# Rank-one attention with keys on partitions: the weighted sums go from VectorE to TensorE

## The reference, cut to what matters

```python
x_avg = jnp.mean(x, axis=(2, 3), keepdims=True)
se_mid = jax.nn.relu(conv1x1(x_avg, se1_w, se1_b))
W_cw = jax.nn.sigmoid(conv1x1(se_mid, se2_w, se2_b))     # a gate per image and channel
g_x = conv1x1(x, g_w, g_b).reshape(b, N)                 # one channel each
theta_x = conv1x1(x, theta_w, theta_b).reshape(b, N)
phi_x = conv1x1(x, phi_w, phi_b).reshape(b, N)
f = theta_x[:, :, None] * phi_x[:, None, :]              # rank one
y = jnp.einsum('bij,bj->bi', jax.nn.softmax(f, axis=-1), g_x)
W_y = conv1x1(y.reshape(b, 1, h, w), W_w, W_b)
inv = bn_gamma / jnp.sqrt(bn_var + BN_EPS)
W_y = (W_y - bn_mean) * inv + bn_beta                    # per channel
return W_cw * W_y + x
```

## Time and profile before

| | |
|---|---|
| median of 3 runs (lowest, highest) | 2871.19 us (2867.90, 2873.26) |
| the profiled execution, its span | 2870.26 us, 2868.5 us |
| busy share of the span: PE, DVE, ACT, POOL | 95%, 76%, 58%, 3% |
| rank-one stage, from its first instruction to the end of the span | 2802.3 to 2868.5 us, 66.2 us |

### The profile page before, as it was taken

One profiled execution on the slowest core, in us unless ns is written; L12 is line 12 of the kernel. 1 busy time (PEld: TensorE's weight loads), 2 busy tenths in 40 slices (PEclk: granted clock), 3 DMA queues, 4 the chain that ended last, 5 costly groups with the idle time before them and its releaser, 6 DMA issues. The chain is left out here.

```text
span 2868.5 us, 45618 instructions
## 1 busy us (share of the span) xinstructions
PE 2717.4 (95%) x19977; PEld 1355.9 (47%) x19977; DVE 2182.4 (76%) x1415; ACT 1672.2 (58%) x2588; POOL 100.4 (3%) x65
## 2 busy tenths in 40 slices
PE   7399999999999999999999999999799999999893
PEld 3334444444444444334444344344578888757551
DVE  5499999999999999999999999998542221234447
ACT  2467776777777767777677777766522222211335
POOL 0000000000000000000000000000440000000004
PEclk9699999999999999999999999999899999999996
DMA  1100000000000000000000000000600000200001
GB/s 69 41 23 22 23 29 9 29 29 16 29 13 32 29 9 29 22 23 29 9 29 29 16 29 18 27 5 1 195 1 0 1 1 2 82 0 1 0 1 59
DMA packets 37607, 72.24 MB, mean 25 GB/s; under 512 B 20960, under 2 KB 21920, under 8 KB 35744
## 3 DMA queue, kind: packets, MB, share of 16 engines
q1 hardware_dynamic: 37344, 69.19, 7.2%
q0 software_dynamic: 64, 0.13, 0.0%
HBM read 60.45 MB, written 8.86 MB: 24 GB/s over the span
## 5 line engine op out<-in xcount | busy, mean ns | idle before, releaser
L734 PE MATMUL l_ps<-mlp_w,W2H 128*64 128x512 f16 x8192 | 1366.5, 392 | 17.2 <-DVE mlp_w L768 17.2
L768 DVE TENSOR_TENSOR mlp_w<-words_x,words_y 128x2048 f32<-128x2048 f32 x512 | 1159.5, 2287 | 66.9 <-PE l_ps L734 66.9
L734 PE MATMUL l_ps<-mlp_w,W2L 128*64 128x512 f16 x4096 | 802.3, 388 | 0.0
L734 PEld LDWEIGHTS l_ps<-mlp_w,W2H 128*64 128x64 f16 x8192 | 455.2, 108 | 549.3 <-issue 116.4
L815 ACT ACTIVATE relu_bottom<-l_ps 128x512 f32<-128x512 f32 x1024 | 612.3, 598 | 79.5 <-PE l_ps L734 1.4
L815 ACT ACTIVATE mlp_w<-l_ps 128x512 f32<-128x512 f32 x684 | 408.8, 598 | 279.7 <-PE l_ps L734 249.7
L752 DVE SCALAR_TENSOR_TENSOR mlp_w<-relu_bottom,sign_ratio,mlp_w 128x2048 f32<-128x2048 f32 x171 | 401.4, 2347 | 7.6 <-ACT relu_bottom L815 7.6
L734 PEld LDWEIGHTS l_ps<-mlp_w,W2L 128*64 128x64 f16 x4096 | 229.0, 109 | 179.7 <-issue 0.8
L815 ACT ACTIVATE relu_top<-l_ps 128x512 f32<-128x512 f32 x340 | 203.2, 598 | 135.7 <-PE l_ps L734 120.8
L723 PE MATMUL l_ps<-y_rows,y_weights_halves 12*128 12x512 bf16 x2048 | 202.4, 385 | 12.1 <-DMA y_rows<-y_pieces 12.1
L752 DVE SCALAR_TENSOR_TENSOR relu_top<-relu_bottom,sign_ratio,relu_top 128x2048 f32<-128x2048 f32 x85 | 199.6, 2349 | 4.0 <-ACT relu_bottom L815 4.0
(11 more groups left out here) (343 smaller groups left out, 2578.8 us busy)
## 6 DMA issues: line engine op xcount, KB each, us to landing
table_pos<-pos_table SPq DMA_DIRECT2D x64, 512.0 KB, 3.6
mlp_w<-in_mlp_w SPq DMA_DIRECT2D x8, 1024.0 KB, 14.0
X<-in_x SPq DMA_DIRECT2D x8, 512.0 KB, 7.6
bias_scratch<-bias_rows SPq DMA_DIRECT2D x64, 64.0 KB, 2.0
mlp_w_hi<-bias_scratch SPq DMA_DIRECT2D x16, 256.0 KB, 3.8
out<-Q SPq DMA_DIRECT2D x8, 512.0 KB, 2.7
y_rows<-y_pieces SPq DMA_DIRECT2D x192, 12.0 KB
xn_b<-in_out_wT SPq DMA_DIRECT2D x1, 1024.0 KB, 6.9
```

What stands on the lines that cost most here:

```text
L734: last = nc.tensor.matmul(out[q][a * DH:(a + 1) * DH, :], w[:, half], h[a][:, :, k], start=False, stop=stop, tile_position=(0, a * DH))
L768: nc.vector.tensor_tensor(hw[i % 3][:, r].rearrange("p (m j) -> p m j", j=J), words_x, words_y[:, 2 * n + r].unsqueeze(1).to_broadcast([P, ...
```

## The change

The rank-one stage is written anew. Keys now stand on partitions, 128 at a time (a round r of 8: 4 per image, as 128 keys of each quarter), and queries lie along the row, 512 at a time. In words:
- The argument of the exponential is a product of TensorE: two rows of keys (phi, and a one) times two rows of queries (theta, and the negative maximum). A round has four such products of 128 x 512, in four row groups of the array; each pair of them fills a double bank, `args`.
- ScalarE takes the exponential of a double bank (128 x 1024) straight from PSUM, without scale, bias or sum, 16 in all.
- The sums over keys are products too, of 32 columns (g, theta, phi, and a row of ones), in four column groups. They add up over the 4 rounds of an image in one bank.
- At the end of an image its bank is copied to SBUF, turned by four transposes, VectorE adds the halves and divides, and four products spread y.
- The largest argument comes from the extremes of phi over rows (two reductions, one set of small products), and `min` of two products of the queries.
- The averages of X are taken in the stage before, by ScalarE: of image 0 in four copies of 128 x 1024, of image 1 in eight of 128 x 512, each behind VectorE's addition. The normalization's coefficients move to the head of the stage before; the sigmoid is made of an exponential and a reciprocal.
- GpSimd only prepares the selecting matrices. VectorE shifts X (8 operations of 128 x 1024) and makes all outputs, in halves of 512 pixels; 16 stores of 256 KB.

The diff, cut to what the prediction speaks of:

```diff
@@ stage_nonlocal, vector: ahead of its own coefficients
+            dve.wait_ge(cs, 2)
+            nc.vector.reciprocal(K.bn_t[:], K.bn_a[:]).then_inc(bn, 1)
...
@@ stage_nonlocal, scalar: in the tail of image 1, and behind the loop
+                            for c in range(2 * t, 2 * t + 2):
+                                act.wait_ge(o_out, NT * CC)
+                                nc.scalar.activation(ex[c % 2], K.X[:, c, 0], ACT.Copy, accum_out=K.av[:, c, 0:1]).then_inc(mean, 1)
+                                act.wait_ge(mean, c + 1)
+                        act.wait_ge(z_mm, b * NT + t + 1)
                         nc.scalar.activation(z[:, t * BANK:(t + 1) * BANK], zps[t][:], ACT.Copy).then_inc(z_out, 1)
+            for i in range(NT * CC):
+                t, c = divmod(i, CC)
+                act.wait_ge(o_out, (B - 1) * NT * CC + i + 1)
+                act.wait_ge(mean, CC + i)
+                nc.scalar.activation(ex[2][:, 0:BANK], K.X[:, c, B - 1, t * BANK:(t + 1) * BANK], ACT.Copy,
+                                     accum_out=(K.av_b[:, c:c + 1] if t else K.av[:, c, 1:2])).then_inc(mean, 1)
@@ stage_rank_one, tensor
+            nc.tensor.matmul(args[0][:, 0], sel_q[:, 0], rows, start=True, stop=True).then_inc(qk_mm, 1)
+            nc.tensor.matmul(args[0][:, 1], sel_k[:, 0], rows, start=True, stop=True).then_inc(qk_mm, 1)
+            pe.wait_ge(ends, 2)
+            for n in range(B * NT):
+                last = nc.tensor.matmul(pps[:, 2 * n:2 * n + 2], sel_m[:, n], mm[:], start=True, stop=True)
...
+            nc.tensor.matmul(gps[:], sel_q[:, 1], rows, start=True, stop=True).then_inc(qk_mm, 1)
+            nc.tensor.matmul(args[2][:, 1], sel_k[:, 1], rows, start=True, stop=True).then_inc(qk_mm, 1)
...
+            def arguments(r):
...
+                for t in range(NT):
+                    k = NT * r + t
+                    if k >= 3:
+                        pe.wait_ge(ex, k - 2)
+                    for u in range(2):
+                        at = 32 * (2 * t + u)
+                        last = nc.tensor.matmul(args[k % 3][:, u], keys[b][at:at + 2, jj * P:(jj + 1) * P], queries[b][at:at + 2, :],
+                                                start=True, stop=True, tile_position=(at, 0))
+                    last.then_inc(a_mm, 1)
+            def weigh(r):
...
+                for t in range(NT):
+                    k = NT * r + t
+                    pe.wait_ge(ex, k + 1)
+                    for u in range(2):
+                        at, n = 32 * (2 * t + u), 32 * (NT * b + u)
+                        last = nc.tensor.matmul(acc[b][at:at + 32, :], rows_t[:, jj, n:n + 32], e[k % EB][:, u],
+                                                start=(jj == 0), stop=(jj == JJ - 1), tile_position=(0, at))
+                last.then_inc(s_mm, 1)
+            def replicate(b, t):
+                pe.wait_ge(col, 4 * (b + 1))
+                if b == 0 and t:
+                    pe.wait_ge(o_out, CC)
+                for r in range(JJ):
+                    last = nc.tensor.matmul(y_ps(b, t)[:, r * P:(r + 1) * P], num[:, b, r, t:t + 1].to_broadcast([P, P]), K.k("ident"),
+                                            start=True, stop=True)
+            for r in range(B * JJ):
+                arguments(r)
+                if r:
+                    weigh(r - 1)
+                if r == JJ + 1:
+                    columns(0)
+                if r == JJ + 2:
+                    replicate(0, 0)
+            weigh(B * JJ - 1)
+            replicate(0, 1)
+            columns(1)
+            for t in range(NT):
+                replicate(1, t)
@@ stage_rank_one, scalar
+            for k in range(TILES):
+                act.wait_ge(a_mm, k + 1)
+                if k >= EB:
+                    act.wait_ge(s_mm, (k - EB) // NT + 1)
+                nc.scalar.activation(e[k % EB], args[k % 3][:], ACT.Exp).then_inc(ex, 1)
@@ stage_rank_one, vector: behind the loop
+            dve.wait_ge(s_mm, JJ)
+            nc.vector.tensor_copy(sums[0], gps[:]).then_inc(s_out, 1)
+            quotient(0)
+            outputs(0, 0)
+            outputs(0, 1)
+            quotient(1)
+            outputs(1, 0)
+            outputs(1, 1)
```

More of the change, by code:

```diff
@@ L1590, in stage_rank_one @@
     d = K.dram
-    se1, se2 = K.se1, K.se2
+    se1, se2, av = K.se1, K.se2, K.av
     room = carver(K.WR)
[L1593 to L1597, removed]
-    gw = sb("gtp_w32", [P, CC, 32])
-    sel = sb("row_select", [P, 2, B * NT, P])
-    th = sb("theta", [P, B * PC])
-    av, mid, gate = sb("avg", [P, CC, B]), sb("se_mid", [SE, B]), sb("gate", [P, CC, B])
@@ L1610, in stage_rank_one @@
[L1610 to L1622, removed]
+    EB, JJ = 6, BANK // P
+    TILES = 2 * B * JJ
+    e = [room([P, 2, BANK]) for _ in range(EB)]
@@ new lines, in stage_rank_one @@
+    rows, rows_t = room([P, BANK]), room([P, JJ, P])
+    queries, keys = [room([P, BANK]) for _ in range(B)], [room([P, BANK]) for _ in range(B)]
+    scaled = [room([P, BANK]) for _ in range(B)]
+    sums = [room([P, BANK]) for _ in range(B)]
+    sel_q, sel_k, sel_m = room([P, B, P]), room([P, B, P]), room([P, B * NT, P])
+    out = carver(K.Q)([P, CC * B, HW])
+    gw = sb("gtp_w32", [P, CC, 32])
+    mid, gate = sb("se_mid", [SE, B]), sb("gate", [P, CC, B])
+    ga, gd = sb("ga", [P, CC, B]), sb("gd", [P, CC, B])
@@ L1677, in _ @@
             last.then_inc(se, 1)
[L1678 to L1682, removed]
+            def arguments(r):
+                b, jj = divmod(r, JJ)
+                pe.wait_ge(q_out, b + 1)
+                pe.wait_ge(k_out, b + 1)
+                for t in range(NT):
+                    k = NT * r + t
+                    if k == 1:
+                        pe.wait_ge(ends, 4)
+                    if k == 2:
+                        pe.wait_ge(t_out, 1)
+                        pe.wait_ge(k_out, 2)
+                    if k >= 3:
[5 more added lines that the diff above has]
+                    last.then_inc(a_mm, 1)
@@ L1747, in _ @@
[L1747 to L1758 removed]
+            dve.wait_ge(g_out, 1)
@@ new lines, in outputs @@
+            def outputs(b, t):
+                dve.wait_ge(y_mm, NT * b + t + 1)
+                dve.wait_ge(xg, CC * (b + 1))
+                part = slice(t * BANK, (t + 1) * BANK)
+                for c in range(CC):
+                    nc.vector.scalar_tensor_tensor(out[:, CC * b + c, part], y_ps(b, t), ga[:, c, b:b + 1], K.X[:, c, b, part],
+                                                   ALU.mult, ALU.add).then_inc(o_out, 1)
+            dve.wait_ge(s_mm, JJ)
+            nc.vector.tensor_copy(sums[0], gps[:]).then_inc(s_out, 1)
@@ L1760, in _ @@
+            quotient(0)
[4 more added lines that the diff above has]
+            outputs(1, 1)
         @block.scalar
         def _(act):
-            nc.scalar.activation(inv[:], K.v("bn_var", 0, CC), ACT.Sqrt, bias=K.eps[:]).then_inc(sq, 1)
-            for i in range(CC * B // 2, CC * B):
-                c, b = divmod(i, B)
-                last = nc.scalar.activation(out[i], K.X[:, c, b], ACT.Copy, accum_out=av[:, c, b:b + 1])
@@ L1767, in _ @@
-            last.then_inc(av_act, 1)
-            act.wait_ge(g_mm, 1)
-            nc.scalar.activation(rows, gps[:], ACT.Identity, bias=K.v("gtp_b")).then_inc(g_out, 1)
-            for i in range(2 * B * NT):
-                b, r = divmod(i, 2 * NT)
-                k, t = divmod(r, NT)
-                act.wait_ge(rep_mm, i + 1)
-                nc.scalar.activation(rep[:, k, b, t * BANK:(t + 1) * BANK], rps[i % 2][:], ACT.Copy).then_inc(rep_out, 1)
+            act.wait_ge(head, 3)
+            act.wait_ge(g_mm, 1)
```

242 lines of the change are left out of this document (125 added, 117 removed).

## The result

| | before | changed |
|---|---|---|
| median of 12 runs each (lowest, highest) | 2869.07 us (2866.95, 2873.26) | 2862.17 us (2859.09, 2868.12) |
| ratio of changed to before, 95% interval | | 0.9978 (0.9970 to 0.9986) |
| the profiled execution, its span | 2870.26 us, 2868.5 us | 2868.04 us, 2866.2 us |
| rank-one stage in the trace | 66.2 us | 57.4 us |

The forecast was 2850.5 us. The change gains, but a third of what was expected. The traces are compared by the length of the stage: where it begins also depends on the three layers ahead, which run the same instructions but for the coefficients and averages, and yet differ between executions by some us (the changed one is 2.2 us behind the one before at the end of the first layer, 2009 us, and 5.8 us from 2054 us on). The profiled execution of the changed kernel, at 2868.04 us, is one of the two longest of its twelve.

The account below looks back on a forecast made before the run. VectorE was taken to bound the loop and ScalarE most of the head. The stage takes 44.9 instead of 66.2 us and begins 0.75 later: 2870.26 - 20.5, plus 0.9 for the median, stated as 2850.5 us; range 2844 to 2864.

Parts of the forecast that it names:

- The start: Stage before: the last average of image 1 lets the rank-one stage begin 0.75 us later; bounds 0 to 5 us.
- The head: Stage's start to first exponential: it starts at 11.3 us, where before it was 20.3; clock left at 1.00.
- The loop's products side by side: Loop: four products of a kind overlap, about 0.86 us, not 3.44 one by one; 2.0 us per round.
- rival B: Loop at half the pace, by the second pair's wait or TensorE at 1.2 GHz: 3.6 us a round, 2863.5; chance 0.22.
- rival C: Loop: row groups don't overlap in float32, arguments 3.44 us a round, no gain, 2870.5; chance 0.06.
- The clock there: Loop: TensorE's granted clock taken as 1.00, as it would be busy 1.9 of 2.0 us.
- Rival D: Loop: both causes of rival B at once, 7.1 us a round, slower at 2891; chance 0.09.
- The insertions: Rounds 5 and 6: image 0's transposes and first spreading find no slack and add 1.8 us.
- The tail: Last sums at 30.1 us to stage's end at 44.9: spreadings, image 1's quotient, outputs of 2.75 and 5.4, store 2.75.
- The sum: Whole stage: 44.9 instead of 66.2 us, beginning 0.75 later, 20.5 us less; 2850.5 us forecast.

Follow-up runs that it names:

- e12: Changed kernel with argument products over 32 rows (30 of zeros) instead of 2 in all rounds, same edit as e1; 2851.34 us, ratio 0.9935 to the kernel before.
- e6: Changed kernel with argument products over 32 rows in rounds 0 to 3 (image 0), 2 rows in rounds 4 to 7; 2850.71 us, run once.
- e11: Changed kernel with argument products over 32 rows in rounds 0 and 1, 2 rows in rounds 2 to 7; 2851.91 us, ratio 0.9938 to the kernel before.
- e1: Changed kernel with argument products over 32 rows (30 of zeros) instead of 2 in all rounds; 2850.76 us, ratio 0.9935 to the kernel before.
- e3: Changed kernel plus one bf16 product over the full array ahead of each round's first pair, arguments still 2 rows; 2863.37 us, ratio 0.9986 to the kernel before.
- e8: Changed kernel with argument products over 32 rows in round 0 alone, 2 rows in rounds 1 to 7; 2863.07 us, ratio 0.9968 to the kernel before.
- e9: Changed kernel with argument products over 2 rows in rounds 0 and 1, 32 rows in rounds 2 to 7; 2854.44 us, run once.

## Why the prediction was wrong, step by step

- *The start*, 0.75 later: 0.74. Right.
- *The head*, first exponential at 11.3: 12.03. The first products end at 4.18 (4.15 forecast). Most of the miss is the small products of line 1694: they hold TensorE 0.81 us from their start to that of the next line (2815.74 to 2816.55), where 0.3 had been taken. The full products were 0.2 longer than forecast and the gate's layer 0.2 shorter. GpSimd was done after 3.25 us (4), and the clock stayed at 1.00 as forecast.
- *The loop's products side by side*: right. In the changed kernel's full rounds all four argument products start within 0.02 us, the wait ahead of the second pair notwithstanding, so the first cause of rival B and rival C are refuted. At the high clock a round's arguments take 1.07 us, or 1.24 where the second pair waits for its exponential, and its sums 1.0 (e12), turns included, where 0.96 each had been summed.
  The Trainium skill, "TensorE: Matmul & The Clock Gate", Part 3, with its 3.07 for four row tiles, gave an estimate of 1.12 us without the turn; e12's rows have 1.07 with the turn in it, where no wait lengthens them.
- *The clock there*, "TensorE will be busy 1.9 of 2.0 us, so I take 1.00". **This is the step that failed.** It was 0.50 for 27 us, and a round took 3.89 instead of 2.0. Rival B named this as its second cause, and said 2863.5 us against the 2862.2 measured. The cost is e12's difference from the changed kernel: 11.0 us in the trace, 10.8 between the medians. The reasoning failed where it read busy time as the clock's measure. The row taken as the model, the first layer's alternation, has argument-like products over 12 rows and a clock of 1.00. It stood next to the right answer: e6 and e11 show that such an alternation does keep a high clock. But the loop's entry doesn't alternate, and its four products over two rows, twice over, were never looked at by themselves. Rival D's own line, that such products are little work, was the better argument.
  The Trainium skill, "TensorE: Matmul & The Clock Gate", Part 1, What's actually happening, says that the clock is set by how busy TensorE has been of late. Busy time as the profile shows it doesn't bear this out: 27.20 of 27.20 us at 0.50 in the changed kernel, 17.20 of 20.10 at 1.00 in e11.
- *The insertions*, 1.8 in all: in e12 the transposes and the spreading delay the exponentials by some 0.7 and 1.0 us. Right. The last exponential ends at 30.6 in e12 (29.1 forecast), of which 0.7 is the head's.
- *The tail*, 14.8 us from the last sums to the end: 13.7 in the changed kernel, since the clock had risen by then and the spreading took 1.17 instead of 1.7. In e12, where the clock is low there as forecast, it is 14.7.
- *The sum*: with wide products all terms hold to 1.5 us together (stage 46.4 for 44.9), and the time is 2850.8 for 2850.5. Of the 11.7 us by which the forecast missed, 10.8 are the clock. That the time agrees to 0.3 us is in part luck: the forecast was taken off a median of 2871.2 us from three runs, and the twelve gave 2869.1. The gain with wide products is 17.4 to 17.6 us (e12, e1), not 20.5. In the traces the stage is 19.8 us shorter and begins 0.74 later; for the rest, the first layer's products start 0.8 to 2.4 us later in all 14 traces of changed kernels than in the one before, and one trace before can't tell whether that is the kernel's or the execution's. The range, 2844 to 2864, held because B was in it.
- One thing in the text ahead of the forecast was imprecise: a round takes 128 keys from each half of the image, for each half of the queries, not "128 keys of each quarter".

Shown: the clock is the cause of the missing gain, 10.8 to 11.0 us of it; widening the argument products of rounds 0 and 1 is enough to keep it; neither their data nor alternation lose it. Open: why one wide product a round (e3) is not enough; whether round 1 alone would do; what brings the clock back ahead of the last rounds in the changed kernel and e3; how long a thin loop can hold a clock that it doesn't win back, as only six such rounds in a row were run; and what makes the head fall early in some executions (e1, e6, e8, e9).

## What to carry to other kernels

A new loop that puts TensorE on the path must be priced at both clocks, and the granted clock read at its entry: here products over 2 rows of a row group kept TensorE busy without holding its clock. If the operands have zeros beside them in a row group, try multiplying the zeros too: here 32 rows instead of 2 cost no time and were worth 11 us. It was enough at the entry, where thin products stand alone.

## What the runs showed of the hardware

- A TensorE that was busy without a gap kept 1.2 GHz for 27 us when the argument products had 2 or 8 rows from the first round on, and had 2.4 GHz when they had 16 or 32, with data or zeros.
- The granted clock depended on what came before: the same thin rounds ran at 1.00 behind two wide ones (e11) or four (e6), and at 0.50 behind thin ones (changed) or, in the trace, one wide one (e8).
- Eight products' instructions with two moving columns and 128 columns of weights (line 1694) took 0.95 us at the high clock, 0.11 from start to start, no less than an instruction with 128 moving columns (128 of them in 14.45 us, 0.11 each). The 0.3 us of the forecast had them at 0.04.
